# Heads of the first attention in TensorE's row quarters, and rotary halves of the causal attention exchanged by DMA

## The chip, the core and the metric

The kernel runs on one core of a Trainium2 chip. TensorE (PE, with PEld for its weight loads), VectorE (DVE), ScalarE (ACT), GpSimd (POOL) and the DMA queue of SyncE (SP) each work through an instruction stream of their own and wait for each other by semaphores. The metric is device time in microseconds, the median of several executions.

## What is computed

A decoder of two layers on x of 8 x 512 x 256, each layer an attention, a cross-attention and a feed-forward block with a residual and a layer norm behind each. The change touches the two attentions, here in their core (H = 16 heads in both; the head width is 16 in L0 and 64 in L1):

```python
# L0
k_rec = (latent_kv @ W_up_k) ; v_rec = (latent_kv @ W_up_v)
scores = einsum('bhqd,bhkd->bhqk', qh, k_rec) / sqrt(d) * decay
out = softmax(scores) @ v_rec ; y = out @ W_o
# L1, rotate_half(x) = concat([-x[d/2:], x[:d/2]])
q = q * cos + rotate_half(q) * sin
k = k * cos + rotate_half(k) * sin
scores = einsum('bhsd,bhtd->bhst', q, k) / sqrt(D) + causal
out = softmax(scores) @ v ; y = out @ wo
```

## The kernel before

The program is six blocks one after the other: `attention("a0")` (L0), a cross-attention, a butterfly FFN, `attention("a1")` (L1), `attention("x1")` (the second cross-attention) and a mixture of experts. `attention` is one function with three kinds. Within it a batch (8 of them) has G = 4 groups of four heads (for a0 and a1), and each group four steps, one for each tile of 128 queries: U = 16 steps a batch. In a0 a step covers 512 keys; in a1 it covers 128, 256, 384 and 512 keys in turn.

The stages of one unit (a group's query tile) are spread over five steps, and each engine's order is written out in its `step`: scores on TensorE and, on VectorE, the read of each head's scores from its PSUM bank with the table and the row maximum (L1030) in step s; the exponential on ScalarE (L828) in s+1; reciprocal and division by the sum (L1003, L1007; GpSimd L869 takes two of the four heads in a0) in s+2; transposes on TensorE (L675) with ScalarE's copies (L820) in s+3; the product with the values (L692, L696) in s+4. Within a step TensorE does the transposes, between them the projections that are due, the values' product, and then the scores. VectorE does the divisions, between them what is due of projections and output rows, and then reads the four scores.

All projections, output rows and scores share four PSUM banks `A` in rotation. `Segment` computes at build time which reader (`dve`, `act`, `rot`, ...) must have emptied a bank before its next use.

The projections of the next group ("items") lie in two of the four steps of a group; `tasks` lists them. Scores are taken in fp32r with each operand split into a high and a low part. In a0 item 0 is the queries: rows 0 to 63 hold the high and 64 to 127 the low parts of four heads (ScalarE L762, VectorE L936). Item 1 is the keys: ScalarE copies the high part `kh`, VectorE subtracts to the low part `kl` (L941), and since each head's 16 rows are picked out by zeros in all others, VectorE multiplies `kh` by four masks (L943) and GpSimd `kl` by the same four (L860), which makes `kpad`; a score is then two matmuls over 128 rows (L636). In a1 each of four items (queries and keys of two head pairs) is projected twice, with the weights and with weights whose rotary halves are swapped (`wqs`, `wupk[:, 1]`, L550 and L553); VectorE multiplies one by cos and one by sin out of PSUM (L954), GpSimd adds (L898), ScalarE rounds to the high part (L766, L768), GpSimd subtracts to the low part (L902, L905).

## Time and profile before

| | us |
|---|---|
| median of 3 runs | 4530.26 (4528.9 to 4539.23) |
| the profiled execution's own time | 4538.19 |
| its span, first to last instruction | 4536.4 |
| L0 attention, first load to last row (about) | 16 to 1020 |
| L1 attention, first load to last row (about) | 1531 to 2734 |
| mean granted TensorE clock | 0.919 |

The page gives each engine's busy share of the span, and the same in 40 slices of 113 us, with the granted clock in tenths of full speed. The groups of instructions give busy time, mean duration of one, and the engine's idle time just before them with what ended it. The timeline gives single instructions. In the trace a matmul of the program in plain fp32 is recorded as two.

### The profile page before, as it was taken

The numbers are of one execution on the slowest core, as the hardware profiler recorded it, in microseconds if no ns is written. First come the engines' busy times: TensorE is split into PE (matmuls) and PEld (weight loads), VectorE is DVE, ScalarE is ACT, GpSimd is POOL, SyncE is SP. The second block draws the span as 40 slices with busy tenths as digits, with TensorE's granted clock in tenths as the row PEclk, the third lists the DMA queues.
The fourth block names the chain that finished last, engine by engine and source line by source line (L and its number), as shares of the span: only waits on it lengthen the run. The fifth ranks groups of instructions, "written<-read, shape, count | busy, mean of one in ns | idle before, by whom it ended". The sixth has DMA issues, their size and how long they took to land. (4 is left out here: it accounts for less than half of the span.)

```text
span 4536.4 us, 81434 instructions
## 1 busy us (share of the span) xinstructions
PE 3707.7 (82%) x25804; PEld 2690.1 (59%) x25805; DVE 2801.6 (62%) x7518; ACT 2074.8 (46%) x4994; POOL 1182.2 (26%) x980
## 2 busy tenths in 40 slices
PE   6888888886869799998989887999999517999980
PEld 4665665665768556655666565777777404666650
DVE  6999989986867476666666655666667321111116
ACT  4777777763342165555555554555556201111110
POOL 3444444433400132332222211112112250000004
PEclk9999999997789899999999998999999658999995
DMA  2000000001020100000000001000000611000013
GB/s 66 6 7 6 6 6 6 1 1 47 14 87 1 60 6 6 1 6 6 6 2 6 1 1 45 7 6 6 9 3 1 226 69 38 29 30 30 28 33 105
DMA packets 80039, 115.50 MB, mean 25 GB/s; under 512 B 14368, under 2 KB 66016, under 8 KB 78944
## 3 DMA queue, kind: packets, MB, share of 16 engines
q1 hardware_dynamic: 73568, 94.56, 6.2%
q0 software_dynamic: 6144, 16.79, 1.2%
q8 instruction: 180, 2.95, 0.3%
q14 instruction: 147, 1.20, 0.1%
HBM read 63.09 MB, written 31.46 MB: 21 GB/s over the span
## 5 line engine op out<-in xcount | busy, mean ns | idle before, releaser
L820 ACT ACTIVATE a_pT<-a_T 128x512 f32<-128x512 f32 (+3 forms) x1024 | 482.5, 513 | 412.8 <-PE a_T L675 405.8
L828 ACT ACTIVATE a_t<-a_t,a_neg 128x512 f32<-128x512 f32 (+3 forms) x1024 | 642.9, 635 | 61.4 <-DVE a_neg L1035 61.1
L675 PE MATMUL a_T<-ident,a_t 128*128 128x128 f32 x3328 | 498.9, 287 | 136.8 <-ACT a_pT L820 56.7
L675 PEld LDWEIGHTS a_T<-ident,a_t 128*128 128x128 f32 x3328 | 388.8, 145 | 307.0 <-issue 197.3
L1007 DVE TENSOR_SCALAR a_t<-a_t,a_inv 128x512 f32<-128x512 f32 (+3 forms) x768 | 559.4, 769 | 9.0
L898 POOL TENSOR_TENSOR a_rsum<-a_rsum,a_rsin 128x512 f32<-128x512 f32 x128 | 170.0, 1328 | 946.5 <-DVE a_rsin L954 946.5
L869 POOL TENSOR_TENSOR a_t<-a_t,a_inv 128x512 f32<-128x512 f32 x256 | 284.1, 1131 | 478.0 <-DVE a_inv L1003 478.0
L1030 DVE CUSTOM_DVE_ANT_0 a_t<-a_A,a_table 128x384 f32<-128x384 f32 (+3 forms) x512 | 225.2, 487 | 233.0 <-PE a_A L647 230.9
L2087 DVE COPY experts_y<-experts_Y 128x256 f32<-128x256 f32 x72 | 30.6, 425 | 513.9 <-PE experts_Y L2025 513.9
L1030 DVE CUSTOM_DVE_ANT_0 a_t<-a_A,a_decay 128x512 f32<-128x512 f32 x512 | 322.1, 683 | 40.6 <-PE a_A L636 38.8
L869 POOL TENSOR_TENSOR x_t<-x_t,x_inv 128x576 f32<-128x576 f32 x128 | 158.1, 1256 | 701.4 <-DVE x_inv L1003 701.4
L636 PE MATMUL a_A<-a_kpad,a_qs 128*128 128x512 f32 x1024 | 287.3, 417 | 32.4 <-DVE a_kl L941 17.6
L2037 PE MATMUL experts_H<-ex_w,experts_xgT 128*128 x576 | 268.1, 608 | 47.6 <-ACT experts_xgT L2064 47.6
L1030 DVE CUSTOM_DVE_ANT_0 x_t<-x_A,x_table,x_mx 128x512 f32<-128x512 f32 x256 | 177.0, 748 | 164.1 <-PE x_A L647 162.6
L2025 PE MATMUL experts_Y<-ex_w,experts_hT 128*128 x1152 | 260.5, 379 | 1.0 <-DVE experts_hT L2096 1.0
L2025 PEld LDWEIGHTS experts_Y<-ex_w,experts_hT 128*128 128x128 f32 x1152 | 218.8, 190 | 61.3 <-issue 35.2
L636 PEld LDWEIGHTS a_A<-a_kpad,a_qs 128*128 128x128 f32 x1024 | 176.6, 189 | 117.7 <-DVE a_mx L1030 31.2
L2128 POOL DMA_INDIRECT combine_got<-moe_results,moe_place x64 | 60.9, 951 | 692.5 <-PEq L2106 658.0
L820 ACT ACTIVATE x_pT<-x_T 128x512 f32<-128x512 f32 (+1 forms) x320 | 176.2, 592 | 125.6 <-PE x_T L675 105.3
L2064 ACT ACTIVATE experts_xgT<-experts_X 128x256 f32<-128x256 f32 x72 | 27.6, 383 | 395.8 <-PE experts_X L2017 395.8
L2037 PEld LDWEIGHTS experts_H<-ex_w,experts_xgT 128*128 128x128 f32 x576 | 104.3, 191 | 169.0 <-issue 169.0
L647 PE MATMUL a_A<-a_khl,a_qhl 64*128 64x128 f32 (+3 forms) x1536 | 168.6, 345 | 39.5 <-DVE a_rsin L954 38.0
(275 smaller groups left out, 7579.7 us busy)
## 6 DMA issues: line engine op xcount, KB each, us to landing
ex_w<-in_f_w_dram SPq DMA_DIRECT2D x16, 1024.0 KB, 13.5
moe_sent<-route_zeros SPq DMA_DIRECT2D x1, 9216.0 KB, 29.7
experts_xg<-moe_sent SPq DMA_DIRECT2D x72, 128.0 KB, 2.0
moe_results<-experts_y SPq DMA_DIRECT2D x72, 128.0 KB, 1.7
a_xin<-x_all SPq DMA_DIRECT2D x16, 512.0 KB, 2.9
x_xin<-x_all SPq DMA_DIRECT2D x16, 512.0 KB, 2.9
x_all<-in_x_dram SPq DMA_DIRECT2D x1, 4096.0 KB, 14.9
out_dram<-x_all SPq DMA_DIRECT2D x8, 512.0 KB
```

The source lines that it names most:

```text
L636: mm = pe.matmul(A[seg.bank(name)][:, 0:keys(u)], qs[:, gp, q], kpad[:, gp, hl, j, 0:keys(u)], start=(n == 0), stop=(n == 1))
L647: mm = pe.matmul(A[seg.bank(at)][:, 0:keys(u)], q_hl[r, gp, ql, j // 2, q], k_hl[r, gp, kl_, j // 2, 0:keys(u)], start=(n == 0), stop=(n = ...
L675: mm = pe.transpose(bank[:, kt, :], t_of(u, j, kt * P, (kt + 1) * P), sh.ident[:])
L820: nc.scalar.activation(to, of, ACT.Copy).then_inc(t_empty, 1)
L828: nc.scalar.activation(t_of(u_e % U, j, 0, n), t_of(u_e % U, j, 0, n), ACT.Exp, bias=neg[:, slot, j:j + 1], scale=SCALE, accum_out=total[: ...
L869: nc.gpsimd.tensor_tensor(t_of(u_n % U, j, 0, NK), t_of(u_n % U, j, 0, NK), inv[:, u_n % 4, j:j + 1].to_broadcast([P, NK]), ALU.mult).then ...
L898: nc.gpsimd.tensor_tensor(rsum[:, i % 2, :], rsum[:, i % 2, :], rsin[:], ALU.add).then_inc(rot_sum, 1)
L1007: nc.vector.tensor_scalar(t_of(u_n % U, j, 0, m), t_of(u_n % U, j, 0, m), inv[:, u_n % 4, j:j + 1], None, ALU.mult).then_inc(normed, 1)
L1030: nc.vector.tensor_tensor_reduce(t_of(s, j, 0, n), A[seg.bank(name)][:, 0:n], table[:, at:at + n], 1.0, mx1[:, slot, j:j + 1] if x1 else L ...
L2025: mm = pe.matmul(Y[parity][:], hT[:, f, :], w2[:, bass.ds(e, 1), f, :].rearrange("p a d -> p (a d)"), start=(f == 0), stop=(f == FT - 1))
L2037: mm = pe.matmul(H[half][:], xgT[:, dt, :], w1[:, bass.ds(e, 1), dt, half * 512:(half + 1) * 512] .rearrange("p a f -> p (a f)"), start=(d ...
L2128: pool.indirect_dma_start(got[:, b % 2, g, :], None, results, bass.IndirectOffsetOnAxis(ap=place[:, b * G + g:b * G + g + 1], axis=0))\
```

## The change

In a0 the masks go. The weights of the queries and keys are laid out on the host so that each head has 32 rows: for the keys its 16 rows twice, for the queries 16 rows that become the high part and 16 that become the low part. ScalarE copies the queries times a column of `halves` that is 1 on the high rows and -1 on the low ones; one VectorE instruction over 128 rows then adds the bank times 0 or 1. Keys are split into `k_hl` by one ScalarE and one VectorE instruction. A score is then two matmuls over 32 rows, with the four heads in the four row quarters of the array: eight matmuls in a row, low parts first, behind a wait for all four banks. GpSimd keeps only its divisions in a0.

In a1 each item is projected once. ScalarE copies it out of PSUM to `raw` (`raw_copy`). SyncE issues four DMAs of 32 partitions (64 KB each) that write it to `raw_swapped` with the rotary halves exchanged. VectorE multiplies `raw` by cos, now from SBUF and at the end of the step instead of between its divisions; GpSimd does four instructions an item instead of two: times sin, add (which writes the rounded high part), subtract, add. `raw` and `rsum` have four buffers, `raw_swapped` two. Swapped weights are no longer loaded, and the next batch's x is loaded from the same SyncE loop, behind the exchange of item 3.

```diff
-            return [((*work, 0), "dve"), ((*work, 1), "rot")]
+            return [(work, "raw")]
...
-            kpad = sb("kpad", [P, 2, 2, 4, NK], F32R)
             qs = sb("qs", [P, 2, S], F32R)
-            kh = sb("kh", [P, S], F32R)
-            kl = sb("kl", [P, S], F32R)
+            q_hi = sb("qhi", [P, 2, S], F32R)
+            k_hl = sb("khl", [P, 2, 2, S], F32R)
...
+            raw = sb("raw", [P, 4, S])
+            raw_swapped = sb("rawswapped", [P, 2, S])
...
-            rsum = sb("rsum", [P, 2, S])
+            rsum = sb("rsum", [P, 4, S])
+            rest = sb("rest", [P, S])
...
+            def swap_halves(b, n):
+                wait_apart(sp, (weights, 16 * len(loads)), (raw_done, b * 4 * G + n + 1), (sin_done, b * 4 * G + n + 1))
+                for k in range(4):
+                    sp.dma_start(raw_swapped[32 * k:32 * k + 32, n % 2, :],
+                                 raw[32 * (k ^ 1):32 * (k ^ 1) + 32, n % 4, :]).then_inc(swapped[n % 2], 16)
+            if a1:
+                with sp.Fori(0, B - 1) as b:
+                    for n in range(4 * G):
+                        swap_halves(b, n)
...
-                    for sw in range(2):
-                        name = (*work, sw)
-                        pe.wait_ge(*seg.empty(turn, name))
-                        bank = A[seg.bank(name)]
-                        if i % 2 == 0:
-                            for t in range(DT):
-                                mm = pe.matmul(bank[:], (wq, wqs)[sw][:, t, col], xT[:, t, :],
-                                               start=(t == 0), stop=(t == DT - 1))
-                        else:
-                            mm = pe.matmul(bank[:], wupk[:, sw, col], lat[:], start=True, stop=True)
-                        mm.then_inc(a_full, 1)
+                    pe.wait_ge(*seg.empty(turn, work))
+                    bank = A[seg.bank(work)]
+                    if i % 2 == 0:
+                        for t in range(DT):
+                            mm = pe.matmul(bank[:], wq[:, t, col], xT[:, t, :], start=(t == 0), stop=(t == DT - 1))
+                    else:
+                        mm = pe.matmul(bank[:], wupk[:, col], lat[:], start=True, stop=True)
+                    mm.then_inc(a_full, 1)
...
-                        pe.wait_ge(kp, b * 4 * G + 4 * (g + 1))
-                        pe.wait_ge(low, b * 4 * G + 4 * (g + 1) + 4)
+                        pe.wait_ge(kl_done, b * G + (g + 1))
...
                 name = ("score", u, j)
                 if a0:
-                    pe.wait_ge(*seg.empty(turn, name))
+                    if j:
+                        return
+                    for h in range(4):
+                        pe.wait_ge(*seg.empty(turn, ("score", u, h)))
                     for n, hl in enumerate((1, 0)):
-                        mm = pe.matmul(A[seg.bank(name)][:, 0:keys(u)], qs[:, gp, q], kpad[:, gp, hl, j, 0:keys(u)],
-                                       start=(n == 0), stop=(n == 1))
-                    mm.then_inc(a_full, 1)
+                        for h in range(4):
+                            r = slice(32 * h, 32 * h + 32)
+                            mm = pe.matmul(A[seg.bank(("score", u, h))][:], qs[r, gp, q], k_hl[r, gp, hl, :],
+                                           start=(n == 0), stop=(n == 1))
+                            if n == 1:
+                                mm.then_inc(a_full, 1)
...
-                    nc.scalar.activation((qs[:, gp, :], kh[:])[i], A[seg.bank(name)][:], ACT.Copy).then_inc(hi, 1)
-                elif a1:
-                    act.wait_ge(rot_sum, b * 4 * G + (4 * g + i + 1 + 2))
-                    if i % 2 == 0:
-                        nc.scalar.activation(q_hl[:, gp, 0, i // 2, :], rsum[:, i % 2, :], ACT.Copy).then_inc(hi, 1)
+                    if i == 0:
+                        nc.scalar.activation(q_hi[:, gp, :], A[seg.bank(name)][:], ACT.Copy,
+                                             scale=halves[:, 0:1]).then_inc(hi, 1)
                     else:
-                        nc.scalar.activation(k_hl[:, gp, 0, i // 2, :], rsum[:, i % 2, :], ACT.Copy).then_inc(hi, 1)
+                        nc.scalar.activation(k_hl[:, gp, 0, :], A[seg.bank(name)][:], ACT.Copy).then_inc(hi, 1)
...
+            def raw_copy(seg, turn, b, work):
+                _, g, i = work
+                n = 4 * g + i
+                act.wait_ge(*seg.full(turn, work))
+                act.wait_ge(low, b * 4 * G + n + 1)
+                nc.scalar.activation(raw[:, n % 4, :], A[seg.bank(work)][:], ACT.Copy).then_inc(raw_done, 1)
...
-            def low_keys(b, g):
-                pool.wait_ge(kl_done, b * G + (g + 1))
-                for j in range(4):
-                    nc.gpsimd.tensor_tensor(kpad[:, g % 2, 1, j, :], kl[:],
-                                            hmask[:, j:j + 1].to_broadcast([P, S]), ALU.mult).then_inc(low, 1)
...
                     for g in range(G):
                         for i in range(4):
                             gp = g % 2
-                            pool.wait_ge(rot_done, b * 4 * G + (4 * g + i + 1))
-                            nc.gpsimd.tensor_tensor(rsum[:, i % 2, :], rsum[:, i % 2, :], rsin[:],
+                            n = 4 * g + i
+                            to = (q_hl, k_hl)[i % 2]
+                            wait_apart(pool, (ready, N_READY), (low, b * LOW_GROUP * G + (n + LOW_GROUP)),
+                                       (swapped[n % 2], b * 32 * 4 * G + 64 * (n // 2 + 1)))
+                            nc.gpsimd.tensor_tensor(rsin[:], raw_swapped[:, n % 2, :], sin[:],
+                                                    ALU.mult).then_inc(sin_done, 1)
+                            pool.wait_ge(sin_done, b * 4 * G + (n + 3))
+                            pool.wait_ge(rot_done, b * 4 * G + (n + 1))
+                            nc.gpsimd.tensor_tensor(to[:, gp, 0, i // 2, :], rsum[:, i, :], rsin[:],
                                                     ALU.add).then_inc(rot_sum, 1)
-                            pool.wait_ge(hi, b * HI_GROUP * G + (HI_GROUP * g + HI_ITEM[i]))
-                            if i % 2 == 0:
-                                nc.gpsimd.tensor_tensor(q_hl[:, gp, 1, i // 2, :], rsum[:, i % 2, :],
-                                                        q_hl[:, gp, 0, i // 2, :], ALU.subtract).then_inc(low, 1)
-                            else:
-                                nc.gpsimd.tensor_tensor(k_hl[:, gp, 1, i // 2, :], rsum[:, i % 2, :],
-                                                        k_hl[:, gp, 0, i // 2, :], ALU.subtract).then_inc(low, 1)
+                            pool.wait_ge(rot_sum, b * 8 * G + (2 * n + 1))
+                            nc.gpsimd.tensor_tensor(rest[:], rsum[:, i, :], to[:, gp, 0, i // 2, :],
+                                                    ALU.subtract).then_inc(rot_sum, 1)
+                            pool.wait_ge(rot_sum, b * 8 * G + (2 * n + 2))
+                            nc.gpsimd.tensor_tensor(to[:, gp, 1, i // 2, :], rest[:], rsin[:],
+                                                    ALU.add).then_inc(low, 1)
...
                     if i == 0:
-                        nc.vector.tensor_tensor(qs[64:128, gp, :], bank[64:128, :], qs[64:128, gp, :],
-                                                ALU.subtract).then_inc(a_dve, 1)
+                        nc.vector.scalar_tensor_tensor(out=qs[:, gp, :], in0=bank[:], scalar=halves[:, 1:2],
+                                                       in1=q_hi[:, gp, :], op0=ALU.mult, op1=ALU.add).then_inc(a_dve, 1)
                     else:
-                        dve.wait_ge(low, b * 4 * G + 4 * (g + 1))
-                        nc.vector.tensor_tensor(kl[:], bank[:], kh[:], ALU.subtract).then_inc(kl_done, 1)
-                        for j in range(4):
-                            nc.vector.tensor_scalar(kpad[:, gp, 0, j, :], kh[:], hmask[:, j:j + 1], None,
-                                                    ALU.mult).then_inc(kp, 1)
+                        nc.vector.tensor_tensor(k_hl[:, gp, 1, :], bank[:], k_hl[:, gp, 0, :],
+                                                ALU.subtract).then_inc(kl_done, 1)
                 elif a1:
-                    dve.wait_ge(low, b * LOW_GROUP * G + (LOW_GROUP * g + (LOW_ITEM[i + 2] if i < 2 else LOW_GROUP + LOW_ITEM[i - 2])))
-                    for sw in range(2):
-                        name = ("item", g, i, sw)
-                        if sw:
-                            dve.wait_ge(rot_sum, b * 4 * G + (4 * g + i + 2))
-                        dve.wait_ge(*seg.full(turn, name))
-                        nc.vector.tensor_tensor((rsum[:, i % 2, :], rsin[:])[sw], A[seg.bank(name)][:], (cos, sin)[sw][:],
-                                                ALU.mult).then_inc((a_dve, rot_done)[sw], 1)
+                    n = 4 * g + i
+                    dve.wait_ge(low, b * 4 * G + (n + 1))
+                    dve.wait_ge(raw_done, b * 4 * G + (n + 1))
+                    nc.vector.tensor_tensor(rsum[:, i, :], raw[:, i, :], cos[:], ALU.mult).then_inc(rot_done, 1)
...
                     for head, work in found:
-                        if head == j:
+                        if head == j and not (a1 and work[0] == "item"):
                             run(seg, turn, b + (work in NEXT and s >= U - QT), work)
                 if own:
@@ -1034,6 +1039,10 @@
                     dve.wait_ge(*seg.emptied(turn, ("score", s, 3)))
                     nc.vector.tensor_scalar(neg[:, slot, :], mx[:, slot, :], -SCALE, None,
                                             ALU.mult).then_inc(negated, 1)
+                if a1:
+                    for _, work in found:
+                        if work[0] == "item":
+                            run(seg, turn, b + (work in NEXT and s >= U - QT), work)```

VectorE in a0, a step with item 1, before (`a_t` are the scores and probabilities, `a_A` the PSUM banks, `a_mx` the maxima):

```order
L1003 RECIPROCAL a_inv<-a_total 128x4
L1007 TENSOR_SCALAR a_t<-a_t,a_inv 128x512 x2
L941 TENSOR_TENSOR a_kl<-a_A,a_kh 128x512
L943 TENSOR_SCALAR a_kpad<-a_kh,a_hmask 128x512 x4
L1030 ISA a_t,a_mx<-a_A,a_decay 128x512
```

and now:

```order
L1040 TENSOR_SCALAR a_neg<-a_mx 128x4
L1008 RECIPROCAL a_inv<-a_total 128x4
L1012 TENSOR_SCALAR a_t<-a_t,a_inv 128x512 x2
L953 TENSOR_TENSOR a_khl<-a_A,a_khl 128x512
L1035 ISA a_t,a_mx<-a_A,a_decay 128x512
```

The four mask products are gone from between the keys' low part and the first read of a score.

TensorE in a0, in the loop over batches, from the values' product to the scores, before (register instructions stand in front of waits):

```order
L692 MATMUL a_O<-a_pT,a_v 32x128 x16
L626 ISA
L627 REGISTER_ALU
L634 REGISTER_ALU
L636 MATMUL a_A<-a_kpad,a_qs 128x512 x2
L634 REGISTER_ALU
L636 MATMUL a_A<-a_kpad,a_qs 128x512 x2
```

and now:

```order
L712 MATMUL a_O<-a_pT,a_v 32x128 x16
L641 ISA
L651 REGISTER_ALU x4
L655 MATMUL a_A<-a_khl,a_qs 128x512 x8
L689 ISA x2
```

Each head's pair of matmuls had its bank's wait in front; now all four waits stand ahead of all eight matmuls.

GpSimd in a1, the first two items of the loop, before:

```order
L898 TENSOR_TENSOR a_rsum<-a_rsum,a_rsin 128x512
L902 TENSOR_TENSOR a_qhl<-a_rsum,a_qhl 128x512
L897 REGISTER_ALU
L898 TENSOR_TENSOR a_rsum<-a_rsum,a_rsin 128x512
L905 TENSOR_TENSOR a_khl<-a_rsum,a_khl 128x512
```

and now the first of them:

```order
L909 TENSOR_TENSOR a_rsin<-a_rawswapped,a_sin 128x512
L911 REGISTER_ALU
L912 REGISTER_ALU
L913 TENSOR_TENSOR a_qhl<-a_rsum,a_rsin 128x512
L915 ISA
L916 TENSOR_TENSOR a_rest<-a_rsum,a_qhl 128x512
L918 REGISTER_ALU
L919 TENSOR_TENSOR a_qhl<-a_rest,a_rsin 128x512
```

Two instructions an item have become four, each behind a wait for the one before it.

## Rows read from the trace of the kernel before

**Rows 1.** The page: busy us (share of span) by engine; granted clock in tenths.

```profile
PE 3707.7 (82%) x25804; PEld 2690.1 (59%) x25805; DVE 2801.6 (62%) x7518; ACT 2074.8 (46%) x4994; POOL 1182.2 (26%) x980
...
PEclk9999999997789899999999998999999658999995
```

**Rows 2.** Three stretches: busy us per engine, granted clock, DMA share, GB/s.

```profile
56.00:1000.00 944.00, 827.38 (x7440) 585.77 (x7444) 869.15 (x1933) 686.25 (x1608) 425.18 (x376) 0.97 0.01 5
1600.00:2700.00 1100.00, 993.50 (x6720) 667.65 (x6720) 723.70 (x2183) 601.22 (x1758) 312.70 (x240) 0.96 0.01 4
1000.00:1200.00 200.00, 137.18 (x891) 122.44 (x884) 147.32 (x294) 65.01 (x100) 79.31 (x56) 0.76 0.12 32
```

**Rows 3.** Line 789, two a batch, after batch 0: ns, first and last start.

```profile
L789 ACT ACTIVATE a_xT<-a_A x14: 585/596/618, 126.2 to 855.6; 128x512 f32<-128x512 f32 x14
L789 ACT ACTIVATE a_xT<-a_A x14: 592/594/597, 1661.6 to 2536.8; 128x512 f32<-128x512 f32 x14
```

**Rows 4.** DVE groups, 56 to 1000 us: busy us, mean ns, idle before.

```profile
L1030 DVE CUSTOM_DVE_ANT_0 a_t<-a_A,a_decay 128x512 f32<-128x512 f32 x508 | 319.6, 683 | 39.9 <-PE a_A L636 38.1 <-PE a_T L675 0.9
...
L943 DVE TENSOR_SCALAR a_kpad<-a_kh,a_hmask 128x512 fp32r<-128x512 f32 x122 | 122.8, 1066 | 0.0
```

**Rows 5.** Timeline of L0: start us, duration us, engine, line, operation, tiles, count.

```profile
408.37 0.18 DVE L1003 RECIPROCAL a_inv<-a_total 128x4 f32<-128x4 f32 x1
...
411.66 4.01 DVE L943 TENSOR_SCALAR a_kpad<-a_kh,a_hmask 128x512 fp32r<-128x512 f32 x4
...
411.81 4.75 POOL L860 TENSOR_TENSOR a_kpad<-a_kl,a_hmask 128x512 fp32r<-128x512 f32 x4 [0.96 <-DVE a_kl L941]
...
418.22 0.17 DVE L1003 RECIPROCAL a_inv<-a_total 128x4 f32<-128x4 f32 x1
...
423.53 0.17 DVE L1003 RECIPROCAL a_inv<-a_total 128x4 f32<-128x4 f32 x1
```

**Rows 6.** Groups of score matmuls, whole span: 128 rows deep; 64 rows deep.

```profile
L636 PE MATMUL a_A<-a_kpad,a_qs 128*128 128x512 f32 x1024 | 287.3, 417 | 32.4 <-DVE a_kl L941 17.6 <-DVE a_mx L1030 6.9 <-DVE a_qs L936 5.3
...
L647 PE MATMUL x_A<-x_khl,x_qhl 64*128 64x512 f32 x768 | 109.3, 411 | 13.9 <-DVE x_mx L1021 13.8
```

**Rows 7.** Timeline of L0: a step with a row add and an item.

```profile
432.95 0.69 DVE L936 TENSOR_TENSOR a_qs<-a_A,a_qs 64x512 fp32r<-64x512 f32 x1
...
433.67 1.19 PE L636 MATMUL a_A<-a_kpad,a_qs 128*128 128x512 f32 x4
...
434.55 0.69 DVE L1030 CUSTOM_DVE_ANT_0 a_t<-a_A,a_decay 128x512 f32<-128x512 f32 x1 [0.91 <-PE a_A L636]
```

**Rows 8.** Groups, whole span: count | busy us, mean ns | idle before, releasers.

```profile
L550 PE MATMUL a_A<-a_xT,a_wqs 128*128 128x512 f32 x256 | 123.7, 606 | 0.0
...
L553 PE MATMUL a_A<-a_lat,a_wupk 128*128 128x512 f32 x256 | 120.4, 593 | 0.0
...
L954 DVE TENSOR_TENSOR a_rsin<-a_A,a_sin 128x512 f32<-128x512 f32 x128 | 87.4, 683 | 48.5 <-PE a_A L550 45.8 <-POOL a_rsum L898 2.1 <-PE a_A L647 0.5
...
L675 PE MATMUL a_T<-ident,a_t 128*128 128x128 f32 x3328 | 498.9, 287 | 136.8 <-ACT a_pT L820 56.7 <-DVE a_t L1007 43.8 <-issue 22.8
```

**Rows 9.** Timeline of L1; lines 943 and 898 over all: ns min/median/max.

```profile
2065.26 1.37 POOL L898 TENSOR_TENSOR a_rsum<-a_rsum,a_rsin 128x512 f32<-128x512 f32 x1 [20.73 <-DVE a_rsin L954]
...
2065.43 1.23 DVE L167 TENSOR_TENSOR a_scratch<-a_scratch 128x4 f32<-128x4 f32 x1
...
L943 DVE TENSOR_SCALAR a_kpad<-a_kh,a_hmask x128: 471/1258/1267, 44.1 to 963.6; 128x512 fp32r<-128x512 f32 x128
...
L898 POOL TENSOR_TENSOR a_rsum<-a_rsum,a_rsin x128: 1255/1276/1442, 1560.5 to 2665.5; 128x512 f32<-128x512 f32 x128
```

**Rows 10.** Waits, 1600 to 2700 us: total us, times, longest us.

```profile
PE a_A L647 <- DVE a_rsin L954: 36.4, 23, 4.1
```

**Rows 11.** DMA issues: KB and us to landing; one issue in the timeline.

```profile
x_ctxT<-in_ctxT_dram SPq DMA_DIRECT2D x8, 64.0 KB, 2.0
...
1533.13 0.61 SPq L487 DMA_DIRECT2D a_wqs<-in_a_w_q_swapped_dram  x1
```

73 lines of the change are left out of this document (34 added, 39 removed).

## Prediction, written before the changed kernel ran

> **What bounds the kernel now.** I read the page's busy shares first: TensorE 82%, VectorE 62% [rows 1]. That is a mean over six blocks, so I cut the two attentions out of the middle of their stretches. In L0 VectorE is busy 869.2 of 944 us (92%), TensorE 88%, ScalarE 73%; in L1 TensorE is busy 993.5 of 1100 us (90%), VectorE 66%, ScalarE 55%, GpSimd 28% [rows 2]. So L0 is VectorE's, with TensorE close behind, and L1 is TensorE's. The length of a batch comes from the copies of x transposed, which are two a batch and lie 0.5 us apart: from batch 1 to batch 7 there are six periods, (855.6 - 0.5 - 126.2)/6 = 121.5 us in L0 and (2536.8 - 0.5 - 1661.6)/6 = 145.8 us in L1 [rows 3]. Eight such batches make 972 and 1166 us, 47% of the run; the rest is not touched.
>
> **L0, what goes.** VectorE's four mask products take 4.01 us in a row, and a step that has them lasts 418.22 - 408.37 = 9.85 us against 423.53 - 418.22 = 5.31 us for the plain one behind it [rows 5]. 122.8 us for 122 of them is 1.01 us each [rows 4], 16 a batch: 16.1 us. GpSimd's four beside them (4.75 us, same rows) end later than VectorE's but nothing on VectorE waits for them; they are worth nothing by themselves. The queries' low part now spans 128 rows instead of 64, at the same 512 columns: nothing.
>
> **L0, the score matmuls.** Today one of 128 rows costs 287.3/1024 = 0.28 us of TensorE's busy time; one of 64 rows, in pairs in the two array halves in the second cross-attention, 109.3/768 = 0.14 us [rows 6]. Quarters aren't in the trace. The bounds are 0.28 (no overlap at all) and 0.07 (each halving of the rows halves the cost); I take 0.1, nearer to what pairs do. TensorE's batch falls from 827.4/944 x 121.5 = 106.5 us by 128 x (0.28 - 0.1) = 23 us to 83 us, and leaves the race.
>
> The Trainium skill (TensorEngine Tiling (Array Packing), Key Properties) says that changing the tiling mode drains TensorE, and every step of L0 now changes into one more mode; it gives no price. If it did cost something like 0.2 us a step, TensorE's 83 us would become 86 and the sum would stay.
>
> **L0, the new wait.** All eight matmuls wait for all four banks. Where nothing else uses a bank, they are free when VectorE has read the last score of the step before, and it then spends 2.7 us on reciprocal and divisions (408.37 to 411.66 less the keys' subtraction of 0.6 [rows 5]): hidden. But an item takes a bank in the rotation, and the fourth score needs that bank back; VectorE empties it as its last act before it reads scores. So in such a step TensorE starts only then. The trace has this once already, where a row add and an item share a step: item read to 433.64, matmuls from 433.67, VectorE idle 0.91 us [rows 7]. Five matmuls come before the first full bank (four low, one high) instead of two, but in quarters: again about 0.9 us (1.7 us if they don't overlap: 5 x 0.28 + 0.3). It holds in eight item steps and one step of values a batch; two have it already: 7 x 0.9 = 6.3 us. Against that, today's waits for scores, 38.1 us in 944 [rows 4], are 4.9 a batch and shrink with the shorter score block: -2. ScalarE used the long steps to catch up: its 686.3/944 x 121.5 = 88.3 us a batch [rows 2] are 5.5 us a step, more than VectorE's plain 5.3, so I give back 0.2 us in each of eight steps: 1.6.
>
> Period: 121.5 - 16.1 + 6.3 - 2 + 1.6 = 111.3 us; 10.2 x 8 = 82 us. The first group's masks stand alone ahead of the first scores (4 us), and four weight issues fewer at 0.6 us [rows 11] make another 2.4, of which I keep 3 + 4 = 7 in all. **L0: -89 us**, bounds -43 (1.7 us stalls) and -139 (none).
>
> **L1, TensorE.** The swapped query projection goes (123.7 us in all) and half of the key projection, 120.4/2 = 60.2 us [rows 8]: 183.9/8 = 23.0 us a batch, from 993.5/1100 x 145.8 = 131.7 to 108.7 us. It idles 14.1 us a batch, and 36.4 us of 1100 are waits for rotated items at a group's start, 4.8 a batch [rows 10]. If these go, TensorE alone gives 118 us.
>
> **L1, GpSimd's chain.** It has four dependent instructions an item instead of two: 1.28 us each, 1.44 at most [rows 9], so about 5.4 us with small gaps, 22 us a group. In front stands the exchange: four issues at 0.6 us and a landing of 2.0 us for 64 KB [rows 11], 4 us. A query projection is 123.7/64 = 1.9 us, a key's half as much, eight transposes 8 x 498.9/3328 = 1.2 us [rows 8], a copy 0.6 [rows 3]. So the first item is raw about 0.6 + 1.9 + 0.6 = 3 us into a group, and the next group's scores are due about 5 us into it, behind 1.2 + 1.9 + 0.9 us and the values' product (about 1). The group must last 3 + 4 + 22 - 5 = 24 us; TensorE's is 118/4 = 29.5. Hidden, by 5 us; at a batch's end the items come one step (6 us) later, and 1 us shows. SyncE is free but for these issues, and the load of x behind item 3 has nine steps to spare.
>
> **L1, VectorE.** It loses sin (16 x 0.68 = 10.9 us a batch [rows 8]). But an instruction of VectorE on SBUF stands while GpSimd runs: one on 4 columns began at 2065.43 and ended at 2066.66, with GpSimd's of 2065.26 + 1.37 = 2066.63; and the mask product takes 0.47 us alone and 1.26 beside GpSimd [rows 9], 0.79 more. GpSimd goes from 32 to 64 instructions a batch, nearly end to end. VectorE's 723.7/1100 x 145.8 = 95.9 us become 85 plus 0 to 25 (32 x 0.79) plus what today's gaps hid: 85 to 122 us, I take 108. That is under TensorE's 118 but so near that the two will wait for each other; I add 6. The Trainium skill (GPSIMD Engine Reference, Key points) names VectorE instructions with two SBUF inputs as contending, and the cos product becomes one: by that, 16 x 0.79 = 13 us of an upper figure is its own.
>
> Period 124 us: 21.8 x 8 = **-174 us**. The start is even: 1.5 MB less to load, a longer GpSimd chain before the first scores, some 4 us each. Bounds -78 (period 136) and -242 (115.5).
>
> **The sum.** 4538.2 - 89 - 174 = 4275 us against the profiled execution's own 4538.2. That one lies 7.9 us above the median; so 4267.
>
> **Rivals.**
> Port bound in L1: every GpSimd instruction holds one of VectorE's, VectorE's 122 us plus its present 14 us of waits make 136 us, L1 gives 78 and the total is 4363. For it: GpSimd is now nearly continuous. Against: reads of PSUM aren't held and fill part of the time. 0.20.
> Quarters don't overlap: L0 gives 43, total 4313. Pairs do overlap, against it. 0.13.
> Both terms whole: L0 -139, L1 -242: 4149. 0.13.
> The clock: TensorE idles more in both blocks. Where it was busy only 69% of a stretch the granted clock was 0.76 [rows 2]. At 0.76 instead of 0.96 L1's 108.7 us become 137 and with 9 us of idle 146, no gain, and L0 keeps some 60: 4470. Against: in L1 TensorE would stay at 108.7 of 124 us, 88%, which L0 shows today at 0.97 [rows 2]. 0.07.
> The slower side: GpSimd's chain in L1 ends last. With x us for an instruction and its gap, a group lasts 2 + 16x us; today it is 145.8/4 = 36.5. The loss eats L0's 89 us when 32 x (2 + 16x - 36.5) exceeds 89, so from x = 2.33 us; at 2.6 the total is 4530 - 89 + 227 = 4668. The longest seen is 1.44. 0.04.
>
> **Chances.** Forecast 0.43, with 4200 to 4330 as its own range. The 80% range, 4160 to 4400, takes in the forecast, the port bound and the missing overlap, and part of the best case. A measurement here can tell about 0.3% (14 us) from no change: faster 0.94, same 0.02, slower 0.04.
>
> **What would show it.** L0's period near 111 us, VectorE's wait for scores near 0.9 us in item steps, score matmuls at 0.07 to 0.14 us; L1's period near 124 us, TensorE's busy time near 109 a batch, GpSimd's four at 1.3 us, next to no wait of the scores for rotated items in the middle groups, VectorE's divisions longer than now. I am wrong if L1's scores wait for GpSimd in every group, if VectorE is the one above 90% in L1, or if the granted clock falls in either block.

## The result, and the profile after

The changed kernel takes 4397.4 us (median of 4 runs, 4397.2 to 4400.5) beside 4530.6 us for the kernel before on the same chip: a ratio of 0.970, with an interval of 0.969 to 0.972. The gain is 133 us, half of the 263 us that the prediction gave as likeliest, and 2.6 us inside the upper end of its range.

The program's blocks are cut by the first load that SyncE issues in each. Timeline of SyncE after (start us, duration, line, tiles):

```profile
16.49 0.59 SPq L486 DMA_DIRECT2D a_xin<-x_all  x1
...
955.40 0.49 SPq L1172 DMA_DIRECT2D x_xin<-x_all  x1
...
1462.48 0.51 SPq L486 DMA_DIRECT2D a_xin<-x_all  x1
...
2590.85 0.55 SPq L486 DMA_DIRECT2D x_xin<-x_all  x1
```

L0 lasts 938.9 us (1006.1 before), the two blocks between 507.1 (508.3), L1 1128.4 (1203.8), the rest 1804.8 (1801.8). So L0 gave 67 us where 89 were forecast, L1 75 where 174 were, and nothing else moved by more than 3.

The page after, and four stretches, each from the first copy of x in batch 1 to the one in batch 7, so that each holds six periods; first L0 and L1 of before, then L0 and L1 of after (columns as in [rows 2]; the bounds are starts of the copies of [rows 3]):

```profile
PE 3439.4 (78%) x25420; PEld 2507.5 (57%) x25421; DVE 2820.9 (64%) x7262; ACT 2073.9 (47%) x4994; POOL 1385.9 (32%) x1108
```

```profile
126.19:855.08 728.89, 638.02 (x5738) 449.72 (x5736) 666.86 (x1485) 526.09 (x1231) 327.12 (x288) 0.97 0.02 6
1661.61:2536.35 874.74, 789.69 (x5258) 530.19 (x5257) 569.33 (x1705) 467.09 (x1363) 250.23 (x192) 0.96 0.01 5
```

```profile
116.64:798.15 681.51, 541.78 (x5736) 362.17 (x5736) 575.81 (x1396) 522.83 (x1231) 213.14 (x192) 0.92 0.02 7
1593.58:2399.68 806.10, 686.63 (x4969) 484.68 (x4969) 684.51 (x1609) 470.78 (x1363) 517.93 (x385) 0.92 0.15 37
```

L0's period is 681.51/6 = 113.6 us (121.5 before; 111.3 forecast). L1's is 806.10/6 = 134.4 us (145.8; 124 forecast). In L1 no engine is busy for more than about 85% of the time: a batch has 114.4 us of TensorE, 114.1 of VectorE, 78.5 of ScalarE and 86.3 of GpSimd, in 134.4. VectorE was to have 108. The six periods of L1 give 68.6 us; the first and the last batch together give only 7.

What VectorE's instructions became in L1, of before (1700 to 2400 us) and after (1650 to 2450 us), by columns:

```profile
L1007 DVE TENSOR_SCALAR a_t<-a_t,a_inv 128x512 f32<-128x512 f32 x80 | 64.6, 844 | 0.7
L1007 DVE TENSOR_SCALAR a_t<-a_t,a_inv 128x384 f32<-128x384 f32 x77 | 39.3, 547 | 0.7
L1007 DVE TENSOR_SCALAR a_t<-a_t,a_inv 128x256 f32<-128x256 f32 x76 | 26.2, 402 | 0.7
```

```profile
L1012 DVE TENSOR_SCALAR a_t<-a_t,a_inv 128x256 f32<-128x256 f32 x96 | 110.3, 1203 | 0.8
L1012 DVE TENSOR_SCALAR a_t<-a_t,a_inv 128x512 f32<-128x512 f32 x96 | 84.7, 928 | 0.9
L960 DVE TENSOR_TENSOR a_rsum<-a_raw,a_cos 128x512 f32<-128x512 f32 x96 | 82.0, 894 | 0.6 <-issue 0.4
...
L1012 DVE TENSOR_SCALAR a_t<-a_t,a_inv 128x384 f32<-128x384 f32 x96 | 56.2, 627 | 0.8
```

A division of 256 columns took 402 ns and takes 1203, three times as long, and more than one of 512. The 380 divisions of these 800 us last from 0.27 to 1.58 us. A piece of the timeline at a batch's end, with the last rotated item, the scores that wait for it, and the next divisions:

```profile
2030.05 1.27 POOL L916 TENSOR_TENSOR a_rest<-a_rsum,a_khl 128x512 f32<-128x512 f32 x1
2031.40 1.27 POOL L919 TENSOR_TENSOR a_khl<-a_rest,a_rsin 128x512 fp32r<-128x512 f32 x1
2032.89 0.89 PE L667 MATMUL a_A<-a_khl,a_qhl 64*128 64x128 f32 x12 [3.09 <-POOL a_khl L919]
...
2036.34 5.54 DVE L1012 TENSOR_SCALAR a_t<-a_t,a_inv 128x512 f32<-128x512 f32 x4
2037.41 1.33 POOL L916 TENSOR_TENSOR a_rest<-a_rsum,a_qhl 128x512 f32<-128x512 f32 x1
2038.83 1.34 POOL L919 TENSOR_TENSOR a_qhl<-a_rest,a_rsin 128x512 fp32r<-128x512 f32 x1
2040.30 1.29 POOL L909 TENSOR_TENSOR a_rsin<-a_rawswapped,a_sin 128x512 f32<-128x512 f32 x1
```

VectorE's four divisions last 5.54 us, 1.38 each, in step with GpSimd's instructions, which begin every 1.4 us. The waits of TensorE in 1650 to 2450 us (total us, times, longest) name VectorE's divisions first; GpSimd's chain shows once a batch, with 18.5/6 = 3 us where I had 1 (the second line answers to [rows 10]):

```profile
PE a_T L695 <- DVE a_t L1012: 56.8, 24, 6.4
PE a_A L667 <- POOL a_khl L919: 18.5, 6, 4.4
```

For L0, the step that the prediction spoke of, a row of the timeline for TensorE and one for VectorE: the eight matmuls wait 3.21 us for the item to be read, then take 0.77 us, and VectorE idles 0.94 us for them (forecast 0.9, from [rows 7]).

```profile
326.83 0.77 PE L655 MATMUL a_A<-a_khl,a_qs 32*128 32x512 f32 x8 [3.21 <-DVE a_khl L953]
...
327.71 0.69 DVE L1035 CUSTOM_DVE_ANT_0 a_t<-a_A,a_decay 128x512 f32<-128x512 f32 x1 [0.94 <-PE a_A L655]
```

### The profile page after: what moved, and what is told of

It is laid out like the page before. It is cut to its first block and busy times, and to the rows that moved or that the text cites. A ratio compares the mean times of both kernels' runs of the same rounds, so it can differ in the third digit from the quotient of the medians.

```text
span 4395.7 us, 81705 instructions
## 1 busy us (share of the span) xinstructions
PE 3439.4 (78%) x25420; PEld 2507.5 (57%) x25421; DVE 2820.9 (64%) x7262; ACT 2073.9 (47%) x4994; POOL 1385.9 (32%) x1108
## 5 line engine op out<-in xcount | busy, mean ns | idle before, releaser
L1012 DVE TENSOR_SCALAR a_t<-a_t,a_inv 128x512 f32<-128x512 f32 (+3 forms) x768 | 719.1, 979 | 9.0
L695 PE MATMUL a_T<-ident,a_t 128*128 128x128 f32 x3328 | 535.3, 300 | 163.8 <-DVE a_t L1012 89.8
L695 PEld LDWEIGHTS a_T<-ident,a_t 128*128 128x128 f32 x3328 | 402.7, 151 | 379.8 <-issue 217.0
L1035 DVE CUSTOM_DVE_ANT_0 a_t<-a_A,a_decay 128x512 f32<-128x512 f32 x512 | 322.7, 685 | 91.0 <-PE a_A L655 89.3
L909 POOL TENSOR_TENSOR a_rsin<-a_rawswapped,a_sin 128x512 f32<-128x512 f32 x128 | 170.1, 1329 | 583.5 <-DMA a_rawswapped<-a_raw 558.7
L1035 DVE CUSTOM_DVE_ANT_0 a_t<-a_A,a_table 128x384 f32<-128x384 f32 (+3 forms) x512 | 224.1, 485 | 128.5 <-PE a_A L667 125.6
L1035 DVE CUSTOM_DVE_ANT_0 x_t<-x_A,x_table,x_mx 128x512 f32<-128x512 f32 x256 | 177.0, 748 | 162.1 <-PE x_A L667 160.5
L2079 ACT ACTIVATE experts_h<-experts_H 128x512 f32<-128x512 f32 x144 | 86.0, 597 | 244.7 <-PE experts_H L2046 244.7
L854 ACT ACTIVATION_READ_ACCUMULATOR a_t<-a_t,a_neg 128x1 f32 x1024 | 197.3, 193 | 0.0
L854 ACT ACTIVATE x_t<-x_t,x_neg 128x576 f32<-128x576 f32 x256 | 194.6, 764 | 0.0
```

The source lines that it names most:

```text
L695: mm = pe.transpose(bank[:, kt, :], t_of(u, j, kt * P, (kt + 1) * P), sh.ident[:])
L854: nc.scalar.activation(t_of(u_e % U, j, 0, n), t_of(u_e % U, j, 0, n), ACT.Exp, bias=neg[:, slot, j:j + 1], scale=SCALE, accum_out=total[: ...
L909: nc.gpsimd.tensor_tensor(rsin[:], raw_swapped[:, n % 2, :], sin[:], ALU.mult).then_inc(sin_done, 1)
L1012: nc.vector.tensor_scalar(t_of(u_n % U, j, 0, m), t_of(u_n % U, j, 0, m), inv[:, u_n % 4, j:j + 1], None, ALU.mult).then_inc(normed, 1)
L1035: nc.vector.tensor_tensor_reduce(t_of(s, j, 0, n), A[seg.bank(name)][:, 0:n], table[:, at:at + n], 1.0, mx1[:, slot, j:j + 1] if x1 else L ...
L2079: nc.scalar.activation(h[:, half * 512:(half + 1) * 512], H[half][:], ACT.Silu).then_inc(h_act, 1)
```

## The experiments

Each is the changed kernel with one edit, unless it says otherwise. All were compared with the kernel before on their own chip (4531 us for the first four, 4514 for the next four, 4512 for the last three), so ratios and blocks are what to compare (between the chips only the last block, the mixture of experts, differs by much: 978 to 982 us in the runs of the first, 961 to 964 in the others). The block columns are as above; "loads" are the code loads of queue 8 in the second cross-attention, which comes back at the end.

| kernel | L0 block, period | L1 block, period | second cross-attention, loads | median, us | ratio |
|---|---|---|---|---|---|
| before | 1006.1, 121.5 | 1203.8, 145.8 | 820.7, 19 | 4530.6 | 1 |
| after | 938.9, 113.6 | 1128.4, 134.4 | 822.4, 19 | 4397.4 | 0.970 |
| L0 alone | 936.0, 113.2 | 1204.2, 146.2 | 825.4, 19 | 4470.2 | 0.986 |
| L1 alone | 1005.6, 121.4 | 1136.5, 135.4 | 840.7, 63 | 4490.0 | 0.990 |
| scores in two pairs | 900.4, 108.4 | 1126.3, 134.2 | 823.8, 19 | 4353.2 | 0.961 |
| scores head by head | 885.9, 105.9 | 1136.3, 135.8 | 842.6, 63 | 4375.7 | 0.966 |
| GpSimd short in L1 | 939.2, 113.4 | 954.5, 114.2 | 822.2, 19 | 4204.7, one run | |
| no exchange in L1 | 938.0, 113.1 | 1119.0, 133.6 | 820.5, 19 | 4364.6, one run | |
| half query projections | 938.1, 113.4 | 1115.6, 133.0 | 842.6, 63 | 4383.6, one run | |
| a head's division on ScalarE | 933.7, 112.8 | 1090.8, 129.5 | 823.0, 19 | 4338.5 | 0.961 |
| three GpSimd instructions | 937.3, 113.4 | 1090.0, 129.3 | 820.0, 19 | 4336.0 | 0.961 |
| head by head, padded | 892.0, 107.7 | 1125.9, 134.2 | 820.4, 19 | 4325.7 | 0.959 |
| all of the last three | 893.5, 108.1 | 1087.8, 129.1 | 821.2, 19 | 4288.3 | 0.950 |

**Each half alone.** `attention` of before was kept beside the new one under another name:

```diff
-        attention(nc, sh, "a1", part("a1_", causal=w["causal"], cos=w["cos"], sin=w["sin"]))
+        attention_before(nc, sh, "a1", part("a1_", causal=w["causal"], cos=w["cos"], sin=w["sin"]))
```

> Only the first attention is changed; the causal attention is that of before. Theory (the two edits are independent; the stage boundaries of the two traces give L0 67 us and L1 75 us, the rest +9 or so): 4530 - 67 = 4463 us, between 4453 and 4475, with L0's period at 113.6 us and L1's at 145.8. Rival (the edits meet through TensorE's clock: L0's lower activity costs later blocks something): L0's period the same, but the blocks behind it longer, total above 4475.

> Only the causal attention is changed; the first attention is that of before. Theory (independent edits): 4530 - 75 = 4455 us, between 4445 and 4467, L1's period at 134.2 us, L0's at 121.5. Rival (L1 gained less than predicted because it starts at a lower granted clock when L0 has been changed): L1's period under 131 us and a total under 4440.

L0 alone: 0.9860 (0.9843 to 0.9876), 61 us, within its bounds, with L1 behind it unmoved (1204.2 us) and the second cross-attention 5 us longer. L1 alone: 0.9901 (0.9884 to 0.9918), only 41 us, a miss for both theories: L1's period is right at 135.4, but the second cross-attention, which no edit touches, is 20 us longer than before. 61 + 41 is 31 us short of the 133 of both; the runs on the code loads, below, offer a reason.

**The wait for four banks (L0).**

```diff
-                    for h in range(4):
-                        pe.wait_ge(*seg.empty(turn, ("score", u, h)))
-                    for n, hl in enumerate((1, 0)):
-                        for h in range(4):
+                    for two in ((0, 1), (2, 3)):
+                        for h in two:
+                            pe.wait_ge(*seg.empty(turn, ("score", u, h)))
+                        for n, hl in enumerate((1, 0)):
+                            for h in two:
```

Head by head, the outer loop runs over `((0,), (1,), (2,), (3,))`.

> The changed kernel, but in L0 the scores come in two pairs: TensorE waits for the banks of heads 0 and 1, multiplies low and high parts of these, then waits for the other two banks. Theory (the wait for all four banks is what VectorE pays in item steps, 0.9 us seven times a batch, and more where the matmuls before it are late): the first full bank comes with only the first two banks free, the stalls fall from 88.3 us in the whole L0 to about 40, the period from 113.6 to 108-110 us, total 4397 - 8 x 5 = about 4360 (4345 to 4375). Rival (VectorE waits because TensorE reaches its scores late, behind transposes and values that wait for divisions, not for the banks): period and total within 0.3%, 4385 to 4410. A matmul is expected at about 0.14 us of busy time instead of 0.097, so 0.7 us a step more of TensorE's time; if that were the limit, it would be slower.

> The changed kernel, but in L0 the scores go head by head, each with its own bank's wait, low part and high part, so that no two quarters can overlap in turn. Theory (a quarter's matmul is cheap only because four run beside one another): the record of a score matmul goes from 0.097 to about 0.25-0.28 us, TensorE's batch from about 90 to 110 us, period 113 to 118, total 4395 to 4435; the stalls for banks are gone but TensorE takes their place. Rival (a matmul of 32 rows is cheap by itself, overlap or not): 0.10 to 0.14 us a matmul, the period at or under that of the pairs.

Pairs give 0.9605 (0.9586 to 0.9625), 44 us less than the changed kernel, 38.5 of them in L0; the total came as the theory said, though VectorE's waits fell to 60.5 us where about 40 were expected. The whole-run groups of VectorE's score read [rows 4], of after, pairs and head by head (idle before, and who ended it):

```profile
L1035 DVE CUSTOM_DVE_ANT_0 a_t<-a_A,a_decay 128x512 f32<-128x512 f32 x512 | 322.7, 685 | 91.0 <-PE a_A L655 89.3
```

```profile
L1036 DVE CUSTOM_DVE_ANT_0 a_t<-a_A,a_decay 128x512 f32<-128x512 f32 x512 | 322.3, 684 | 61.9 <-PE a_A L656 60.5
```

```profile
L1036 DVE CUSTOM_DVE_ANT_0 a_t<-a_A,a_decay 128x512 f32<-128x512 f32 x512 | 322.2, 683 | 45.9 <-PE a_A L656 44.4
```

89.3 us become 60.5 and 44.4: the four-bank order is worth 45 us of VectorE's idle time, 5.6 a batch, and 7.7 us of the period (5.9 in the padded run below). Both edits change two things at once, the wait and the number of matmuls ahead of the first full bank: five, three and two of them. From the prices below these take about 0.48, 0.41 and 0.28 us, an estimate, so in the steps where VectorE waits up to 0.2 us of the difference is the order of the matmuls and the rest the wait; no run has the one without the other. Head by head was a miss (its rival came true), and an instructive one. The groups of the score matmuls [rows 6], of the same three:

```profile
L655 PE MATMUL a_A<-a_khl,a_qs 32*128 32x512 f32 x1024 | 99.0, 461 | 109.3 <-DVE a_khl L953 49.7 <-DVE a_qs L950 43.8 <-DVE a_v L995 13.0
```

```profile
L656 PE MATMUL a_A<-a_khl,a_qs 32*128 32x512 f32 x1024 | 139.9, 453 | 47.6 <-DVE a_qs L951 29.0 <-DVE a_khl L954 15.5 <-DVE a_v L996 2.7
```

```profile
L656 PE MATMUL a_A<-a_khl,a_qs 32*128 32x512 f32 x1024 | 142.2, 451 | 42.6 <-DVE a_qs L951 27.1 <-DVE a_khl L954 15.1
```

Four quarters in turn cost 99.0/1024 = 0.097 us a matmul, which is the 0.1 of the prediction. But one quarter twice and then the next costs 0.139, about the same as pairs (0.137), not 0.28. So most of the price falls without four in turn, and the 0.04 us saved by it (43 us of TensorE in all of L0) were bought with a wait that costs VectorE more. L0's block fell by 53 us to 886.

**What holds L1.** Three runs take one thing away each. GpSimd's four instructions on 128 of 512 columns (for each of them; the output differs):

```diff
-                            nc.gpsimd.tensor_tensor(rsin[:], raw_swapped[:, n % 2, :], sin[:],
+                            nc.gpsimd.tensor_tensor(rsin[:, 0:P], raw_swapped[:, n % 2, 0:P], sin[:, 0:P],
```

> The changed kernel, but GpSimd's four instructions an item in L1 take 128 of the 512 columns (the rotated rows of the other columns are left at zero), so the output is another; count, order and waits stay. Theory (the port is what L1 did not gain: VectorE's instructions on SBUF stand while GpSimd runs): GpSimd's busy time falls from 87 to about 30 us a batch, VectorE's from 114 to 90-95, the mean division of 512 columns from 946 ns to under 800, L1's period from 134.3 to 120-125 us, near TensorE's 115. Rival (VectorE's longer divisions are paid in its idle time, and L1 is set by TensorE and its waits): the period falls by under 4 us though VectorE's busy time falls all the same.

No exchange (the wait on `swapped` becomes one on `raw_done`):

```diff
-                            nc.gpsimd.tensor_tensor(rsin[:], raw_swapped[:, n % 2, :], sin[:],
+                            nc.gpsimd.tensor_tensor(rsin[:], raw[:, n % 4, :], sin[:],
```

> The changed kernel, but without the 512 exchanges of 64 KB: GpSimd multiplies the unexchanged copy by sin as soon as ScalarE has written it, so the output is another. Theory (exchange hidden, 5 us of slack a group): L1's period 134.3 to 132-134, TensorE's wait for the last rotated item goes from 3 us a batch to 0-2. Rival (the exchange's 4 us stand on the path of every group): 4 x 4 = 16 us a batch less, period about 118-122.

A shorter query projection:

```diff
-                        for t in range(DT):
-                            mm = pe.matmul(bank[:], wq[:, t, col], xT[:, t, :], start=(t == 0), stop=(t == DT - 1))
+                        mm = pe.matmul(bank[:], wq[:, 0, col], xT[:, 0, :], start=True, stop=True)
```

> The changed kernel, but a query projection in L1 multiplies only the first of the row tiles of x (one matmul instead of DT), so the output is another; TensorE has about 8 x 1 us (half of 1.9 us each, with two tiles) less a batch. Theory (VectorE and the coupling set L1, TensorE is no longer the bound): the period falls by 0 to 3 us. Rival (TensorE bound, at its 115 of 134 us): it falls by the whole 7 to 8 us, to about 126.

The first decides it. Its stretch of six periods in L1, and its divisions (1700 to 2200 us):

```profile
1565.24:2250.31 685.07, 646.05 (x4970) 458.43 (x4969) 441.04 (x1609) 465.53 (x1363) 197.02 (x384) 0.98 0.17 43
```

```profile
L1014 DVE TENSOR_SCALAR a_t<-a_t,a_inv 128x512 f32<-128x512 f32 x70 | 35.2, 549 | 0.6
L1014 DVE TENSOR_SCALAR a_t<-a_t,a_inv 128x384 f32<-128x384 f32 x72 | 26.8, 415 | 0.6
L1014 DVE TENSOR_SCALAR a_t<-a_t,a_inv 128x256 f32<-128x256 f32 x70 | 22.7, 382 | 0.6
```

With the same number of instructions (1609), the same waits and the same exchanges, VectorE's batch falls from 114.1 to 73.5 us and the period from 134.4 to 114.2, below what I expected; TensorE is then busy for 107.7 of 114.2 us. The block of L1 loses 174 us. GpSimd's own busy time falls by 53.5 us a batch (86.3 to 32.8), so each us taken from GpSimd gave VectorE 0.76 us back: 40.6 us a batch, or 0.63 for each of GpSimd's 64 instructions. That VectorE's instructions became shorter is shown; how much of the period is due to that is argued, since the run shortens GpSimd's chain as well as the hold. The other two leave little for the chain: without the exchange the period is 133.6, and TensorE's wait for the last rotated item falls from 18.5 to 5.0 us in 800 while its wait for divisions stays, 59.1 where it was 56.8. With TensorE relieved of 5.7 us a batch (686.63 to 652.31 in six) the period falls by 1.4, and by no more than 3 if the code loads described at the end lengthened that run's L1 as they did another's (135.8 against 134.2). So the exchange is hidden, and TensorE's own work is not what L1 waits for. The rivals of both runs, 118 to 122 and 126 us, are out.

**Two remedies.** Every fourth head's division goes to ScalarE:

```diff
+                u_n = s - LAG_N
+                if a1 and s < U and (own if u_n >= 0 else prev):
+                    act.wait_ge(inverted, b * U + (u_n + 1))
+                    for j in (3,):
+                        m = keys(u_n % U)
+                        nc.scalar.activation(t_of(u_n % U, j, 0, m), t_of(u_n % U, j, 0, m), ACT.Copy,
+                                             scale=inv[:, u_n % 4, j:j + 1]).then_inc(normed_pool, 1)
```

> The changed kernel, but in L1 the division of every fourth head is done by ScalarE, behind its exponentials, by a scale read from the column of reciprocals; TensorE's transpose of that head waits for it. VectorE loses 16 divisions a batch, 16 x 0.88 = 14 us, ScalarE (80 of 134 us busy) gains 16 x about 0.55 = 9 us. Theory (VectorE is L1's bound): the period falls from 134.3 by 7 to 11 us to 123-127, the total to 4310-4340. Rival (ScalarE, now waiting for reciprocals in its order, delays the copies that TensorE's next transposes need): the period within 3 us of 134.3, the total 4375-4420.

Or GpSimd has three instructions, with the rounding on ScalarE at the end of the next step:

```diff
-                            nc.gpsimd.tensor_tensor(rest[:], rsum[:, i, :], to[:, gp, 0, i // 2, :],
-                                                    ALU.subtract).then_inc(rot_sum, 1)
...
+                nc.scalar.activation((q_hl, k_hl)[i % 2][:, g % 2, 0, i // 2, :], rsum[:, i, :], ACT.Copy).then_inc(hi, 1)
```

> The changed kernel, but an item of L1 costs GpSimd three instructions instead of four: sin product, sum (of two items), then the low part, with the rounding to the high part done by ScalarE at the end of the step behind. 16 GpSimd instructions a batch less (87 to 66 us), 16 copies of 0.6 us more on ScalarE (80 to 90 of 134 us). Theory (each GpSimd us costs the period 0.375 us, from the run with short columns: 20.1 us of period for 54 us of GpSimd): 21 x 0.375 = 8 us a batch less, period about 126, total about 4335 beside a before of 4530 (ratio 0.957). Rival (ScalarE, which works in order, now waits for GpSimd's sums and holds up the copies behind it): period 132 to 138, ratio 0.967 to 0.975.

Both are faster than the changed kernel: 0.9614 (0.9598 to 0.9630) each, some 40 us. Both missed their period, 129.5 and 129.3 us where 123 to 127 and about 126 were expected. VectorE's busy time fell from 684.51 us in six periods to 622.28 and 610.36, or 10.4 and 12.4 us a batch (14 had been expected of the first). TensorE's waits in 1650 to 2450 us, first in the changed kernel (beside its 56.8 us for divisions, above), then with three GpSimd instructions, then with a head's division on ScalarE:

```profile
PE a_T L695 <- ACT a_pT L845: 6.3, 18, 0.4
```

```profile
PE a_T L694 <- ACT a_pT L849: 51.0, 27, 3.8
PE a_T L694 <- DVE a_t L1024: 21.8, 14, 4.3
```

```profile
PE a_T L696 <- DVE a_t L1020: 45.4, 14, 6.4
PE a_T L696 <- ACT a_pT L846: 10.6, 30, 0.8
```

With three instructions VectorE's part fell from 56.8 to 21.8 us, and ScalarE's rose from 6.3 to 51.0: ScalarE stands in its order for GpSimd's sums (34.4 us in the same 800 before its copies to `a_khl`) while transposes wait to be copied. With the division on ScalarE this is not so. TensorE waits for ScalarE hardly more than before, and still 45.4 us for VectorE's divisions; why that period stopped at 129.5 us is left open.

**Code loads, and all together.**

```diff
+            for _ in range(112 if a1 else 0):
+                pe.wait_ge(pv, 2)
```

> The kernel with L0's scores head by head, and 112 waits on TensorE that are met already, ahead of the causal attention: they lengthen TensorE's program by 56 instructions, so that the loops of L1 and of the second cross-attention lie where they lie in the changed kernel. Theory (these two blocks were 10 and 18 us longer in that kernel because TensorE's code was loaded 63 times instead of 19 times in the second cross-attention): the loads are back at 19, the block at 822 us, the total about 4376 - 28 = 4348 (ratio 0.9595). Rival (the two blocks were longer for another reason, such as what L0 leaves behind): 4370 to 4385, ratio 0.9655, the padding costing nothing.

> Scores head by head in L0, the 112 met waits, every fourth head's division of L1 on ScalarE, and three GpSimd instructions an item. If the gains add up: L0 886 us (as head by head), L1's period 134.3 - 4.8 - 8 = 121.5, about the 118 at which TensorE would stand alone, total 4348 - 39 - 60 = about 4250 beside a before of 4530 (ratio 0.938). Rival (ScalarE becomes the bound of L1, with 80 + 9 + 10 = 99 us and waits in its order): period 126 to 132, ratio 0.945 to 0.955.

The padding did what its theory said: the second cross-attention is back at 19 loads and 820.4 us, 22 less, and L1 at 1125.9, 10 less. The ratio is 0.9593 (0.9574 to 0.9612) where 0.9595 was expected; that it agrees so closely is partly luck, since L0, with the same code, took 892.0 us here and 885.9 without the padding, which I can't explain. All three together: 0.9501 (0.9482 to 0.9521), 4288 us, the fastest kernel of the study, and inside what the rival allowed (period 126 to 132, ratio 0.945 to 0.955). L1 is at 129.1, hardly shorter than with either remedy alone, so their gains do not add: TensorE's wait for ScalarE is 63.6 us in 800. ScalarE is busy for only 92.7 of the 129.1 us, so it is its order that counts and not its busy time.

## Why the prediction was half right

The time lies 2.6 us inside the 80% range, and that is luck: it is outside the 4200 to 4330 that I gave the forecast itself, L0's term was 22 us too large and L1's 99 us. Of my three signs of being wrong one came, the fall of the granted clock, in both blocks (0.97 and 0.96 to 0.92). VectorE is busy for 85% of L1, not above 90%, and the scores wait for GpSimd once a batch, not in every group.

**What bounds, and the mechanism:** right. L0 was VectorE's, whose busy time fell by 15.2 us a batch (666.86 to 575.81 in six) where I had 16.1 for the masks; L1 went from TensorE to a coupled state in which VectorE waits behind GpSimd.

**GpSimd's masks, "worth nothing by themselves":** this does not fit the rows. A mask product takes VectorE 0.47 us alone [rows 9] and took 1.0 us beside GpSimd's masks [rows 5], so by an estimate from these 16 x 0.53, some 8 of the 16 us, were time for which GpSimd held VectorE. No run takes GpSimd's masks out alone.

**Score matmul 0.1 us:** right, 0.097.

**The new wait in L0:** right in kind and per step (0.94 us), and a little small in sum: I had 4.9 + 6.3 - 2 = 9.2 us a batch, measured were 89.3/8 = 11.2. The 2 us of difference are most of the 2.3 by which the period missed; the rest is VectorE's busy time, which fell 0.9 us less than forecast, against the wait for ScalarE, which rose by 1.0 instead of 1.6. I took the wait as given by the change, and did not ask what it bought: it costs 6 to 8 us a batch (see the runs above) and saves time on an engine that I had just taken out of the race.

**TensorE's busy time:** low by 7.3 us in L0 and 5.7 in L1, 90.3 (541.78/6) against 83 and 114.4 against 108.7. In L1 the instructions were counted rightly, since the run with short GpSimd instructions has 107.7, and the granted clock made the rest: its mean was 0.92, mostly the 2.4 GHz level with parts at 1.2, where it had been 0.96, and 0.98 in that run. In L0 the clock fell too, from 0.97 to 0.92, but no run has L0's new instructions at the old clock, so there it is the likely cause and not shown. TensorE was busy for 79 and 85% of the two stretches where it had been busy for 88 and 90%. The clock rival had named this; in L1 the fall was 0.04 where that rival took 0.20.

**VectorE's 108 us in L1:** measured 114.1, inside my 85 to 122. I took VectorE's 85 us as the base and 23 for GpSimd's new instructions; from that base the new ones cost 29. The base was not free of holds either: with GpSimd's instructions cut to a quarter VectorE has 73.5 us, so the whole hold of all 64 is at least 40.6 (the short ones may hold too, for less).

**The coupling, "I add 6":** the choice between forecast and port bound hung on it. In my terms TensorE was to be busy for 108.7 us and idle for 9.3 + 6 = 15.3; it was busy for 114.4 and idle for 20.0. So of the 10.4 us by which the period missed, 5.7 are its busy time, at the lower clock, and 4.7 its waits; with short GpSimd instructions both are gone (107.7 and 6.5). The waits came because a held instruction lasts about as long as GpSimd's, whatever its own length, so the hold doesn't follow the steps' size: four divisions of 256 columns grow from 1.6 to 4.8 us. TensorE then waits for divisions, up to 6.4 us at a time and 56.8 us in 800. In other steps VectorE waits for TensorE's scores, least in the steps of 512 keys and most in those of 128 (1650 to 2450 us, the score reads by columns):

```profile
L1035 DVE CUSTOM_DVE_ANT_0 a_t<-a_A,a_table 128x512 f32<-128x512 f32 x96 | 60.3, 681 | 2.6 <-PE a_A L667 2.6
L1035 DVE CUSTOM_DVE_ANT_0 a_t<-a_A,a_table 128x384 f32<-128x384 f32 x95 | 47.2, 552 | 13.4 <-PE a_A L667 13.2
L1035 DVE CUSTOM_DVE_ANT_0 a_t<-a_A,a_table 128x256 f32<-128x256 f32 x96 | 35.4, 418 | 23.1 <-PE a_A L667 21.7 <-issue 1.3
L1035 DVE CUSTOM_DVE_ANT_0 a_t<-a_A,a_table 128x128 f32<-128x128 f32 x96 | 25.4, 290 | 35.1 <-PE a_A L667 34.1 <-issue 0.9
```

The two take turns, and an average over a batch can't show that. The rival "port bound in L1" had this mechanism, and its period of 136 is near the 134.4 that came, but the number is partly luck. It added 122 us of VectorE and "its present 14 us of waits"; measured were 114.1 and 20.3. In the rows the 14 us are TensorE's idle time (145.8 - 131.7), while VectorE's was 145.8 - 95.9 = 49.9, and of its 122 us the last 12 stand in no row.

**"x 8":** in both blocks I multiplied a period's gain by eight batches. The six full periods gave 47 and 69 us; the rest of the blocks 20 and 7 us, where I had 28 and 43. It is not a rule that the ends give nothing: with short GpSimd instructions L1's ends gave 249 - 190 = 60 us. Of the 99 us that L1 missed, 62 are the period and 36 the ends.

**Hidden:** the exchange was (0.8 us of period), and GpSimd's chain except for 3 us a batch. The slower side never came near: the longest of GpSimd's instructions in L1 took 1.73 us, against the 2.33 from which it would have decided. A quarter's matmul did not stay at 0.28 us, so the rival of the missing overlap fell too.

The Trainium skill (SBUF — State Buffer, SBUF: two separate sides) says that VectorE and GpSimd share one pair of ports under an exclusive lock, which the one that starts first keeps for its whole instruction; the trace agrees, with four divisions of 1.38 us each in step with GpSimd's instructions of 1.3. On VectorE's side it names instructions in a two-port mode or with two SBUF inputs. The short run agrees as far as it goes: the division and the cos product, which has two SBUF inputs, are the ones that shrank (928 to 549 ns and 894 to 705, for 512 columns), while the score read, whose scores come from PSUM, did not (681 ns in the changed kernel, 687 in the short run). In which mode the division runs, no trace here shows.

## What to carry to other kernels

Before work is moved to GpSimd, count its time as time that VectorE may lose too: here 54 us a batch less of GpSimd gave VectorE 41 us back, and 21 us less (the run with three instructions) 12. The number of instructions alone did not decide, since the run with short ones kept all 64; it shows nearly the whole price at once (174 us here). And the loss falls on short instructions of VectorE as well as on long ones.

The same rows show a hold that neither the prediction nor any run touched. In L0, which is VectorE's, two of a step's four divisions are GpSimd's (110 to 750 us, the changed kernel):

```profile
L1012 DVE TENSOR_SCALAR a_t<-a_t,a_inv 128x512 f32<-128x512 f32 x180 | 216.8, 1230 | 3.2
L884 POOL TENSOR_TENSOR a_t<-a_t,a_inv 128x512 f32<-128x512 f32 x180 | 199.8, 1132 | 437.0 <-DVE a_inv L1008 437.0
```

VectorE's two cost it 2.46 us a step, while the shortest of them in L0 took 0.47 us each. By these numbers all four on VectorE alone would take 1.9 us, less than the two do now; this is an estimate and untried.

When a change saves time on one engine by a wait for several buffers, ask which engine pays for the wait; four banks at once saved TensorE 43 us and cost L0 some 50. Count a loop's gain over its full periods, and look at its first and last turn by themselves.
